# A graph network on one core: one-hot rows made by VectorE, four to a comparison, in place of ScalarE

## The chip, the cores and the metric

One core of a Trainium2 chip runs the whole program. The metric is the device time of one execution in microseconds (us). TensorE is PE in the rows, VectorE DVE, ScalarE ACT, GpSimd POOL; SyncE (SP) issues most transfers.

## The reference

12500 nodes with 128 features, 200000 edges `(src, dst)` sorted by `dst`. Three layers add up neighbours' rows, then one attention layer weights them; layer norms close both parts.

```python
def _L0_gnn_ref(h, src, dst, W1, b1, W2, b2, eps):
    for l in range(W1.shape[0]):                      # three layers
        agg = jax.ops.segment_sum(h[src], dst, num_segments=n)
        z = (1.0 + eps[l]) * h + agg
        hid = jnp.maximum(z @ W1[l] + b1[l], 0.0)
        h = hid @ W2[l] + b2[l]
    return h

def _L1_gnn_ref(h, w, a, src, dst):
    hi, hj = h[src], h[dst]
    e = jnp.matmul(jax.nn.leaky_relu(jnp.matmul(jnp.concatenate([hi, hj], -1), w), 0.2), a)
    exp_e = jnp.exp(e)
    att = exp_e / jax.ops.segment_sum(exp_e, src, num_segments=N)[src]
    return jax.ops.segment_sum(hi * att, dst, num_segments=N)

x = _layernorm(x + _L0_gnn_ref(...))
x = _layernorm(x + _L1_gnn_ref(...))
```

## The kernel before

The nodes lie in 98 windows of 128; their running sums stay in SBUF as `agg`, features on partitions, nodes along the free dimension. The edges lie in tiles of 128 which belong to one window each, except one tile in 16 (the first of a turn) that may reach into the next window. 1568 tiles make 98 turns of 16; a turn is four quads of four tiles. There are four stages that gather: three layers (first rows of `x`, then of `table_g`), then the scores (rows of `table_p`); a last stage of 104 turns gathers little. Between the layers PE, ACT and DVE make the next table by blocks of four windows, and SP stores it.

In a layer the engines work on a tile in this order:

- SP refills the indices (L560) and POOL issues one indirect transfer per tile (L766), which brings 128 rows into a ring of 32 slots. At every fourth gather POOL waits until the quad that had the slots has been multiplied (`rows_used`).
- ACT makes the tile's one-hot matrix from `rel_t`, each edge's place in its window: |iota - rel| by L923 (one instruction per tile), then relu(1 - that) for a quad at once by L933, and by L932 for the second 128 columns of a turn's first tile. L941 copies a turn's 16 columns of `rel_t` with the sign turned. The one-hots go to `span_hot`, four buffers of a quad (`IN_HAND`).
- PE multiplies the rows with the one-hots into PSUM (L1178), a quad in two banks, after waits for DVE's additions, for the one-hots (L1174, L1176) and for the rows.
- DVE adds each tile's sums into its window of `agg` (L1585; L1589 for a turn's second window). It loads 8 window numbers at a time into registers (L468), and for each addition a step of its sequencer (L1562) multiplies the window by 128 and writes the address. Each addition waits for the one before.

In the scores DVE and ACT work on the gathered rows and SP keeps them in HBM; POOL's ring slots come free by SP's L599. PE uses window numbers there. In the last stage DVE weights (L1818, L1829), makes a low part's one-hots (L1810) and adds 16 tiles per turn (L1571), again with addresses made by L1562. Order on each engine is the order of the code; loops are hardware loops.

Of the kernel before, what the change touches and what calls it, by code (L numbers as in the profile page):

```python
# [81 lines left out]
FIRST_A = LAYERS * T2  # L82
# [32 lines left out]
def gnn(nc, x, src, dst, w1, b1, w2, b2, eps, w, a, out):  # L115
    ctx = ExitStack()
    with ctx:
# [34 lines left out]
        def per_tile16(at):  # L152
# [56 lines left out]
        span_at = 6 * QROWS  # L209
        span_away = [big[:, span_at + k * QUAD * 2 * P:span_at + (k + 1) * QUAD * 2 * P].rearrange("p (t n) -> p t n", t=QUAD)  # L210
                     for k in range(2)]
        assert span_at + 2 * QUAD * 2 * P <= CHUNKS * PW
# [48 lines left out]
        one_col = sb("one_col", [P, 1], f32)  # L261
        rel_now = sb("rel_now", [P, TPI], f32)
# [74 lines left out]
        iota_ps = ps[7][:, 0:P]  # L337
        a_ps = ps[6][:, 0:PW]
# [35 lines left out]
        rel_set = sem("rel_set")  # L374
        span_ready = sem("span_ready")
# [14 lines left out]
        hot_ready = sem("hot_ready")  # L390
        rows_used = sem("rows_used")
# [67 lines left out]
        USED = RING  # L459

# [5 lines left out]
        def load_windows(first, engine, n=HALF, of=tile_win):  # L466

            _, values = nc.values_load_multi_w_load_instructions(  # L468
                of[0:1, ds(first, n)], engines=(engine,), min_val=0, max_val=WINS - 1,
                skip_runtime_bounds_check_because="a tile's window, by its making")  # L470
            return list(values)

        def sums_at(q, j):

            return ps[2 * q + j // 2][:, (j % 2) * 2 * P:(j % 2 + 1) * 2 * P]
# [51 lines left out]
        def _(sp):  # L527
# [186 lines left out]
        def _(pool):  # L714
# [137 lines left out]
        def _(act):  # L852
# [61 lines left out]
            def one_hots(l):  # L914

                def distances(turn, q):

                    quad = turn * IN_HAND + q
                    act.wait_ge(hot_ready, 2 + l * QUADS2 + quad - 1)
                    for j in range(QUAD):  # L920
                        t = q * QUAD + j
                        wide = 2 * P if t == 0 else P
                        ins = act.activation(span_away[q % 2][:, j, 0:wide], iota_w[:, 0:wide], ACT.Abs, bias=rel_now[:, t:t + 1])  # L923
                    ins.then_inc(span_ready, 1)

                def hots(turn, q):

                    quad = turn * IN_HAND + q
                    act.wait_ge(span_ready, l * QUADS2 + quad + 1)
                    act.wait_ge(rows_used, USED + l * T2 + quad * QUAD - (IN_HAND - 1) * QUAD)  # L930
                    if q == 0:
                        act.activation(span_hot[q][:, 0, P:2 * P], span_away[q % 2][:, 0, P:2 * P], ACT.Relu, bias=one_col[:, :], scale=-1.0)  # L932
# [3 lines left out]
                with act.Fori(0, TURNS2) as i:  # L936
                    if l:
                        act.wait_ge(span_ready, l * QUADS2 + i * IN_HAND)
                    else:
                        act.wait_ge(hot_ready, 2 + i * IN_HAND)  # L940
                    act.activation(rel_now[:, :], rel_t[:, ds(i * TPI, TPI)], ACT.Copy, scale=-1.0).then_inc(rel_set, 1)  # L941
                    act.wait_ge(rel_set, l * TURNS2 + i + 1)
                    for q in range(IN_HAND):
                        distances(i, q)
                        if q >= 1:
                            hots(i, q - 1)
                    hots(i, IN_HAND - 1)

            act.sem_inc(hot_ready, 2)
            act.wait_ge(g_taken, 2 * QUADS)  # L950
            one_hots(0)
# [4 lines left out]
            one_hots(1)  # L956
            act.wait_ge(added[QUAD - 1], IN_HAND + 2 * QUADS2)
# [4 lines left out]
            one_hots(2)  # L962
            act.wait_ge(added[QUAD - 1], IN_HAND + 3 * QUADS2)
# [128 lines left out]
        def _(pe):  # L1092
            pe.sem_inc(rows_used, USED)
            pe.sem_inc(den_added, 8)
# [71 lines left out]
            def sum_rows(no):  # L1166

                with pe.Fori(0, RINGS2) as i:
                    for t in range(RING):
                        q = (t // QUAD) % IN_HAND  # L1170
                        if t % QUAD == 0:
                            quad = no * QUADS2 + i * (RING // QUAD) + t // QUAD
                            pe.wait_ge(added[QUAD - 1], quad + 1)
                            pe.wait_ge(hot_ready, quad + 3)  # L1174
# [3 lines left out]
                        ins = pe.matmul(sums_at(q, t % QUAD)[:, 0:wide], ring[:, t, :], span_hot[q][:, t % QUAD, 0:wide],  # L1178
                                        start=True, stop=True)
                        if t % QUAD == QUAD - 1:  # L1180
                            ins.then_inc(rows_used, QUAD)
                pe.wait_ge(added[QUAD - 1], (no + 1) * QUADS2 + IN_HAND)
# [149 lines left out]
        def _(dve):  # L1332
            own = Count(dve, dve_own)
            dve.sem_inc(bank_free, HALF)
            for j in range(QUAD):
                dve.sem_inc(added[j], IN_HAND)
# [553 lines left out]
```

## Time and profile before

| | us |
|---|---|
| median of three runs | 9327.69 |
| the runs | 9326.17 to 9331.99 |
| span of the profiled execution | 10761.6 |
| POOL busy in it | 6943.5 |
| PE / DVE / ACT busy in it | 4749.1 / 3994.5 / 3909.3 |

The span runs from the first to the last instruction of one profiled execution; it is 1433.9 us longer than the median of the runs, and all durations below are read from it. Small instructions of an engine's sequencer, such as address steps, are not counted as busy; the chain of work that ended last names them with a q behind the engine (DVEq). "remote" and "another core or an unknown queue" stand for a release whose source the profile does not find.

### The profile page before, as it was taken

To read this page: it belongs to the slowest core of one execution; us is meant where nothing else is said; L and a number is where in the kernel's file an instruction comes from. 1 tells how busy PE (TensorE), PEld (TensorE's weight loads), DVE (VectorE), ACT (ScalarE), POOL (GpSimd) and SP (SyncE) were. 2 spreads that over 40 slices of the span, in tenths; PEclk is the share of its full clock that TensorE was granted. 3 is DMA by queue.
4 is the path that set the end of the run, shared out by engine and by line. 5 is a ranking of instruction groups with operands and counts; after the bars stand their busy time and mean duration, and the time that the engine had idled before them with its cause. 6 is when DMAs were issued, how large, how long until landed. Compare 5 with 4: busy or idle time off the path is not lost.

```text
span 10761.6 us, 137184 instructions
## 1 busy us (share of the span) xinstructions
PE 4749.1 (44%) x27323; PEld 4216.7 (39%) x27324; DVE 3994.5 (37%) x13681; ACT 3909.3 (36%) x11178; POOL 6943.5 (65%) x7392
## 2 busy tenths in 40 slices
PE   3323222343322323342333332256666666667776
PEld 2222222232222222232222222256666666666665
DVE  2222222222222222222222222256556655568888
ACT  3333333333333333333333333322222222237777
POOL 5666666656666666656666666646666666658886
PEclk6555555566555555565555555677778777789998
DMA  3111111122111111121111111145555555544444
GB/s 81 45 46 45 45 46 45 46 59 51 45 45 46 45 46 46 45 65 47 46 45 46 45 46 45 46 139 149 146 147 148 148 147 147 146 132 138 138 139 133
DMA packets 918236, 875.96 MB, mean 81 GB/s; under 512 B 253109, under 2 KB 764001, under 8 KB 918175
## 3 DMA queue, kind: packets, MB, share of 16 engines
q0 software_dynamic: 239728, 516.96, 18.5%
q1 hardware_dynamic: 614765, 259.14, 8.7%
q10 hardware_dynamic: 63698, 99.36, 3.3%
q8 instruction: 15, 0.25, 0.0%
q14 instruction: 30, 0.25, 0.0%
HBM read 734.15 MB, written 137.96 MB: 81 GB/s over the span
## 4 chain that ended last, share of the span: by engine, by line
issue 26%; another core or an unknown queue 23%; DVE 20%; DVEq 17%; PE 11%; ACT 2%; DMA 0%; ACTq 0%; POOL 0%; SPq 0%; POOLq 0%
DVE agg L1585 8%; DVEq L1562 7%; DVEq L468 5%; DVE agg L1571 4%; PE psum L1251 4%; PE psum L1276 2%; DVEq L1580 2%; PE psum L1270 2%; DVE big L1818 2%; DVEq L1593 1%; DVE work L1692 1%; DVE work L1699 1%; PE psum L1178 1%; DVE work L1689 1%
## 5 line engine op out<-in xcount | busy, mean ns | idle before, releaser
L1178 PE MATMUL psum<-work,rows 128*128 128x128 f32 (+1 forms) x9408 | 2056.2, 394 | 4728.1 <-DVE agg L1585 2465.2
L766 POOL DMA_INDIRECT rows<-table_g,idx_now x3136 | 2966.9, 946 | 1688.0 <-issue 1061.4
L1178 PEld LDWEIGHTS psum<-work,rows 128*128 128x128 f32 x9408 | 1825.5, 284 | 4959.6 <-issue 2822.9
L1585 DVE TENSOR_TENSOR agg<-agg,psum 128x128 f32 x4704 | 1351.4, 287 | 5323.6 <-remote 3145.3
L933 ACT ACTIVATE work<-big,one_col 128x512 f32<-128x512 f32 x1176 | 817.9, 710 | 3315.9 <-remote 2837.2
L766 POOL DMA_INDIRECT rows<-in_x,idx_now x1568 | 1483.3, 946 | 799.3 <-issue 467.6
L923 ACT ACTIVATE big<-iota_w,rel_now 128x128 f32<-128x128 f32 (+1 forms) x4704 | 1501.6, 396 | 429.5 <-remote 345.0
L766 POOL DMA_INDIRECT rows<-table_p,idx_now x784 | 764.3, 975 | 480.8 <-SPq L599 254.9
L1010 ACT ACTIVATE work<-psum 128x256 f32<-128x256 f32 x784 | 295.2, 387 | 1864.9 <-remote 1129.9
L1251 PE MATMUL psum<-work 128*128 128x98 f32 x3168 | 624.3, 362 | 689.0 <-DVE work L1692 362.4
L1251 PEld LDWEIGHTS psum<-work 128*128 128x128 f32 x3168 | 569.5, 269 | 741.3 <-DVE work L1692 392.9
L1270 PE MATMUL psum<-big,work 128*128 x3136 | 773.0, 334 | 153.4 <-DVE work L1718 112.3
L766 POOL DMA_INDIRECT work<-table_p,idx_now x588 | 576.3, 980 | 377.2 <-SPq L599 214.5
L1312 PE MATMUL psum<-rows,hot 128*128 128x128 f32 x3328 | 660.4, 326 | 236.9 <-ACT hot L1049 197.2
L1270 PEld LDWEIGHTS psum<-big,work 128*128 128x128 f32 x3136 | 607.5, 240 | 182.2 <-issue 178.5
L1312 PEld LDWEIGHTS psum<-rows,hot 128*128 128x128 f32 x3328 | 496.8, 207 | 382.8 <-ACT hot L1049 250.0
L828 POOL TENSOR_SCALAR hot<-iota_w,big 128x128 f32<-128x128 f32 x624 | 490.4, 790 | 85.1 <-DVE big L1829 63.5
L836 POOL DMA_INDIRECT big<-table_r,idx_now x416 | 412.4, 991 | 147.6 <-issue 99.0
L1571 DVE TENSOR_TENSOR agg<-agg,psum 128x128 f32 x1664 | 476.8, 287 | 51.8 <-PE psum L1312 1.2
L1049 ACT ACTIVATE hot<-big 128x128 f32<-128x128 f32 x1040 | 477.9, 478 | 0.0
L1689 DVE TENSOR_TENSOR work<-psum,hilo 128x392 f32<-128x392 f32 x396 | 222.5, 562 | 556.7 <-remote 406.1
L1699 DVE TENSOR_TENSOR work<-work,psum 128x516 f32<-128x516 f32 x392 | 270.1, 689 | 421.9 <-ACT work L1011 320.8
(211 smaller groups left out, 5718.4 us busy)
## 6 DMA issues: line engine op xcount, KB each, us to landing
rows<-x_of SPq DMA_DIRECT2D x415, 256.0 KB
rows<-table_g,idx_now POOLq DMA_INDIRECT x3136
work<-rel_rows ACTq DMA_DIRECT2D x196, 256.0 KB
x_of<-rows SPq DMA_DIRECT2D x196, 256.0 KB
big<-lo_rows ACTq DMA_DIRECT2D x208, 192.0 KB
x_of<-work SPq DMA_DIRECT2D x147, 256.0 KB
rows<-in_x,idx_now POOLq DMA_INDIRECT x1568
idx_now<-src_t SPq DMA_DIRECT2D x784, 4.0 KB
```

Source lines behind the costliest of these rows:

```text
L468: _, values = nc.values_load_multi_w_load_instructions(of[0:1, ds(first, n)], engines=(engine,), min_val=0, max_val=WINS - 1, skip_runtime ...
L766: pool.indirect_dma_start(out=to, out_offset=None, in_=table, in_offset=bass.IndirectOffsetOnAxis(ap=idx_now[:, at:at + 1], axis=0)) \
L828: pool.tensor_scalar(hot[:, j, :], iota_f[:, :], scalars[:, h, 1, 0, j:j + 1], scalars[:, h, 0, 0, j:j + 1], ALU.is_equal, ALU.mult).then_ ...
L923: ins = act.activation(span_away[q % 2][:, j, 0:wide], iota_w[:, 0:wide], ACT.Abs, bias=rel_now[:, t:t + 1])
L933: act.activation(span_hot[q][:, :, 0:P], span_away[q % 2][:, :, 0:P], ACT.Relu, bias=one_col[:, :], scale=-1.0).then_inc(hot_ready, 1)
L1178: ins = pe.matmul(sums_at(q, t % QUAD)[:, 0:wide], ring[:, t, :], span_hot[q][:, t % QUAD, 0:wide], start=True, stop=True)
L1251: ins = pe.matmul(den_ps, den_hot[:, t % 8, 1, :], den_hot[:, t % 8, 0, 0:HI], start=False, stop=False)
L1270: pe.matmul(sums, hot_t[:, t // QUAD, (t % QUAD) * P:(t % QUAD + 1) * P], q_rows[:, ds(windows[t - h * HALF] * PW, PW)], start=True, stop= ...
L1312: pe.matmul(ps[j // 2][:, (j % 2) * D:(j % 2 + 1) * D], hot[:, j, :], row_of(h * HALF + j, D), start=True, stop=True).then_inc(rows_used, 1)
L1562: dve.lower_ap(to)
L1571: dve.tensor_tensor(to, to, sums, ALU.add).then_inc(bank_free, 1)
L1585: dve.tensor_tensor(to, to, sums_at(q, j)[:, 0:P], ALU.add).then_inc(added[j], 1)
```

## The change

- In the layers DVE makes the one-hots, by comparing a counting row with `rel_t`: one comparison of 128x512 for a quad, and one of 128x128 more for the second window of a turn's first tile. The counting row is copied into PSUM bank 7 ahead of each layer (`iota_2`). ACT has nothing to do in the layers' loops.
- The one-hots for quad q+2 are made just before DVE waits for the sums of quad q; those of the first two quads ahead of the loop. The last turn is taken out of the loop.
- A quad's sums lie in one PSUM bank; a turn's first tile has bank 4 (`IN_HAND`), since it is twice as wide.
- PE counts multiplied quads by a new semaphore, `quads_summed`, one per quad instead of `rows_used` plus 4. It, `added[3]` and `hot_ready` start at such values that PE and DVE wait for the same number at all of them. SP and POOL wait for `quads_summed` in the layers.
- Window numbers are multiplied by 128 once for all tiles (`scale_windows`, one partition, 1664 numbers), ahead of the layers and again ahead of the last stage. DVE loads these and makes the addresses of 8 or 9 tiles at a time. The second window's addition now comes first in its turn.

```diff
-            def one_hots(l):                       # ACT
-                def distances(turn, q):
...
-                        ins = act.activation(span_away[q % 2][:, j, 0:wide], iota_w[:, 0:wide], ACT.Abs, bias=rel_now[:, t:t + 1])
...
-                    act.activation(span_hot[q][:, :, 0:P], span_away[q % 2][:, :, 0:P], ACT.Relu, bias=one_col[:, :],
-                                   scale=-1.0).then_inc(hot_ready, 1)
...
                 def used(lap, lane):               # SP
-                    sp.wait_ge(rows_used, USED + no * T2 + lap * LAP + (lane + 1) * HALF)
+                    sp.wait_ge(quads_summed, Q_USED + no * QUADS2 + lap * (LAP // QUAD) + (lane + 1) * (HALF // QUAD))
...
-                            pool.wait_ge(rows_used, USED - RING + no * T2 + lap * LAP + lane * HALF + j + QUAD)
+                            pool.wait_ge(quads_summed, no * QUADS2 + lap * (LAP // QUAD) + (lane * HALF + j) // QUAD + 1)
...
-                            pe.wait_ge(added[QUAD - 1], quad + 1)
-                            pe.wait_ge(hot_ready, quad + 3)
+                            pe.wait_ge(added[QUAD - 1], Q_USED + quad + 2 - IN_HAND)
+                            pe.wait_ge(hot_ready, Q_USED + quad + 2 - IN_HAND)
...
-                            ins.then_inc(rows_used, QUAD)
+                            ins.then_inc(quads_summed, 1)
...
+            def scale_windows():                   # DVE, this and all below
+
+                own.add(dve.tensor_single_scalar(sums_at_win, tile_win, D.bit_length() - 1, ALU.logical_shift_left))
+                own.wait()
...
+            def one_hots(q, first):
...
+                if q == 0:
+                    dve.tensor_tensor(span_hot[q][:, 0, P:2 * P], iota_2[:, P:2 * P], rel_t[:, ds(first, 1)].to_broadcast([P, P]),
+                                      ALU.is_equal)
+                dve.tensor_tensor(span_hot[q][:, :, 0:P], iota_2[:, 0:P].rearrange("p (o n) -> p o n", o=1).to_broadcast([P, QUAD, P]),
+                                  wide(rel_t[:, ds(first, QUAD)], QUAD), ALU.is_equal).then_inc(hot_ready, 1)
+
+            def add_quad(q, value, sums_to, second_to):
+
+                dve.wait_ge(quads_summed, value)
+                if q == 0:
+                    dve.tensor_tensor(second_to, second_to, sums_at(0, 0, 2 * P)[:, P:2 * P], ALU.add).then_inc(seconds_added, IN_HAND)
+                    dve.wait_ge(seconds_added, value + IN_HAND - 1)
...
+                    to = sums_to[(q % 2) * QUAD + j]
+                    if j:
+                        dve.wait_ge(added[j - 1], value)
+                    dve.tensor_tensor(to, to, sums_at(q, j), ALU.add).then_inc(added[j], 1)
...
+            def sum_turn(l, turn, hots_from):
...
+                    windows = load_sums_at(turn * TPI + h * HALF)
+                    second = load_sums_at(turn + REAL, 1) if h == 0 else []
+                    sums_to = [sums_of(window) for window in windows + second]
+                    for q in range(2 * h, 2 * h + 2):
+                        dve.wait_ge(added[QUAD - 1], values[q])
+                        if q < hots_from:
+                            one_hots((q + 2) % IN_HAND, turn * TPI + (q + 2) * QUAD)
+                        add_quad(q, values[q], sums_to, sums_to[-1])
...
+                own.add(dve.tensor_copy(iota_2, iota_w[:, :]))
+                own.wait()
+                for q in range(2):
+                    one_hots(q, q * QUAD)
+                with dve.Fori(0, TURNS2 - 1) as i:
+                    sum_turn(l, i, IN_HAND)
+                sum_turn(l, TURNS2 - 1, 2)
...
+            scale_windows()                        # also between the scores and the last stage
```

DVE in a layer's loop, a turn's first quad before (ISA is a step of the sequencer; `exp_rel` holds `rel_t`):

```order
L1562 ISA
L1580 ISA [waits rows_used]
L1585 TENSOR_TENSOR agg<-agg,psum 128x128 [waits added3]
L1562 ISA
L1589 TENSOR_TENSOR agg<-agg,psum 128x128 [waits added0]
L1562 ISA
L1585 TENSOR_TENSOR agg<-agg,psum 128x128 [waits seconds_added]
L1562 ISA
L1585 TENSOR_TENSOR agg<-agg,psum 128x128 [waits added1]
L1562 ISA
L1585 TENSOR_TENSOR agg<-agg,psum 128x128 [waits added2]
```

The same quad on DVE in the changed kernel:

```order
L1537 ISA x3
L1556 ISA [waits added3]
L1556 TENSOR_TENSOR work<-psum,exp_rel 128x4x128
L1563 TENSOR_TENSOR agg<-agg,psum 128x128 [waits quads_summed]
L1569 TENSOR_TENSOR agg<-agg,psum 128x128 [waits seconds_added]
L1569 TENSOR_TENSOR agg<-agg,psum 128x128 [waits added0]
L1569 TENSOR_TENSOR agg<-agg,psum 128x128 [waits added1]
L1569 TENSOR_TENSOR agg<-agg,psum 128x128 [waits added2]
```

The address steps have moved ahead of a half turn, and one comparison stands before the wait for the quad's sums.

DVE between the scores and the last stage, in the changed kernel:

```order
L1766 TENSOR_SCALAR exp_rel<-exp_rel 128x98
L1768 COPY src_t<-src_t 128x98 [waits rows_used]
L1771 TENSOR_SCALAR big<-src_t 128x1664 [waits dve_own]
L1529 TENSOR_SCALAR big<-hot 1x1664 [waits dve_own]
L1774 CAST big<-big 128x1664 [waits dve_own]
L1776 COPY idx_now<-src_t 128x2 x2
```

L1529, the scaling of the windows, is new there; the others stood in a row before, as L1768 to L1777.

## Rows read from the trace of the kernel before

**Rows 1.** Layer 0, scores, last stage: length; busy us of PE, PEld, DVE, ACT, POOL.
```profile
77.60:2363.00 2285.40, 684.96 (x3177) 605.88 (x3175) 479.65 (x1675) 812.34 (x2173) 1483.26 (x1568) 0.58 0.18 45
...
7132.50:9627.00 2494.50, 1606.49 (x9670) 1519.10 (x9670) 1479.14 (x3372) 519.42 (x2056) 1531.35 (x1571) 0.78 0.54 145
9627.00:10714.00 1087.00, 849.52 (x7036) 698.43 (x7036) 877.20 (x4562) 817.38 (x2287) 899.97 (x1037) 0.91 0.48 137
```

**Rows 2.** Timeline of POOL in layer 1: start, duration, instruction, idle before.
```profile
3003.15 0.95 POOL L766 DMA_INDIRECT rows<-table_g,idx_now  x1 [0.30 <-issue]
...
3014.41 0.95 POOL L766 DMA_INDIRECT rows<-table_g,idx_now  x1 [0.31 <-issue]
```

**Rows 3.** Timeline of POOL, then of DVE, in the scores.
```profile
8000.96 0.96 POOL L766 DMA_INDIRECT hot<-table_p,idx_now  x1 [0.30 <-issue]
...
8001.15 0.68 DVE L1690 TENSOR_TENSOR work<-psum,hilo 128x512 f32<-128x512 f32 x1
8001.74 0.55 DVE L1692 TENSOR_TENSOR work<-work,psum 128x392 f32<-128x392 f32 x1
```

**Rows 4.** POOL's gathers: durations, first and last start; layers 0, 1, 2, scores.
```profile
L766 POOL DMA_INDIRECT rows<-in_x,idx_now x1568: 942/947/1217, 77.6 to 2345.6; - x196
...
L766 POOL DMA_INDIRECT rows<-table_g,idx_now x1568: 942/947/1457, 2412.1 to 4679.7; - x196
...
L766 POOL DMA_INDIRECT rows<-table_g,idx_now x1568: 942/947/962, 4730.7 to 7000.5; - x196
...
L766 POOL DMA_INDIRECT rows<-table_p,idx_now x784: 954/960/1193, 7132.5 to 9549.2; - x196
L766 POOL DMA_INDIRECT work<-table_p,idx_now x588: 954/960/1199, 7157.9 to 9573.9; - x196
```

**Rows 5.** Who waited for whom, the layers: us in total, times, longest.
```profile
POOL rows L766 <- remote: 935.7, 232, 6.7
```

**Rows 6.** Timeline of all engines in layer 1, a late release.
```profile
3009.60 2.47 PE L1178 MATMUL psum<-work,rows 128*128 128x256 f32 x8 [13.69 <-issue]
...
3018.16 1.25 DVE L1585 TENSOR_TENSOR agg<-agg,psum 128x128 f32 x4 [8.80 <-remote]
```

**Rows 7.** Chain of work, layer 1, a slow stretch and a fast one: start, us, what.
```profile
3008.32 0.70 DVEq L1562
...
3029.30 0.07 DVEq L1562
```

**Rows 8.** The same chain over one undisturbed turn of DVE, first and last.
```profile
3027.97 0.14 issue
...
3035.71 0.65 issue
```

**Rows 9.** Timeline of DVE between the scores and the last stage.
```profile
9616.03 1.03 DVE L1773 TENSOR_SCALAR big<-src_t 128x1664 int32<-128x1664 int32 x1
```

**Rows 10.** Timeline of ACT ahead of layer 0, making its weights.
```profile
96.26 0.28 ACT L889 ACTIVATE w<-psum 128x128 f32<-128x128 f32 x1 [11.51 <-remote]
```

**Rows 11.** Timelines of ACT and DVE between layers 0 and 1.
```profile
2410.88 1.64 ACT L905 ACTIVATE agg<-psum,agg_bias,eps 128x512 f32<-128x512 f32 x2 [0.36 <-PE psum L1201]
...
2443.53 1.89 DVE L1602 CAST big<-big 128x1664 int16<-128x1664 f32 x1 [34.93 <-issue]
...
2448.30 1.03 DVE L1607 CAST big<-big 128x1664 int16<-128x1664 int32 x1
```

**Rows 12.** Timeline of DVE in the last stage.
```profile
10003.70 2.53 DVE L1571 TENSOR_TENSOR agg<-agg,psum 128x128 f32 x8
```

**Rows 13.** Timeline of the scores, then of POOL beside DVE's L1607.
```profile
8021.64 0.48 DVE L1718 TENSOR_SCALAR work<-work,node_c 128x512 f32<-128x512 int16 x1
8021.88 1.07 POOL L766 DMA_INDIRECT work<-table_p,idx_now  x1 [0.30 <-issue]
...
8023.25 1.15 POOL L766 DMA_INDIRECT work<-table_p,idx_now  x1 [0.30 <-issue]
...
2448.69 1.46 POOL L766 DMA_INDIRECT rows<-table_g,idx_now  x1 [0.30 <-issue]
```

More of the change, by code:

```diff
@@ L208, in gnn @@
         assert QUAD * ROW + QROWS <= 2 * T2
[L209 to L212, printed above, removed]
+        sums_at_win = big[0:1, CHUNKS * PW - QROWS:CHUNKS * PW].bitcast(i32)
+        assert max(6 * QROWS, rest_at + HI + P) <= CHUNKS * PW - QROWS
         e_src = rows[:, 0:QROWS].bitcast(i32).rearrange("p (r e) -> p r e", r=RG)
@@ L337, in gnn @@
         iota_ps = ps[7][:, 0:P]
+        iota_2 = ps[7][:, 0:2 * P]
         a_ps = ps[6][:, 0:PW]
@@ L390, in gnn @@
         hot_ready = sem("hot_ready")
+        quads_summed = sem("quads_summed")
         rows_used = sem("rows_used")
@@ L459, in gnn, with load_windows, load_sums_at, sums_at @@
         USED = RING
+        Q_USED = RING // QUAD
         def stand_alone(eng):
             eng.sem_inc(passed, 1)
-        def load_windows(first, engine, n=HALF, of=tile_win):
+        def load_windows(first, engine, n=HALF):
             _, values = nc.values_load_multi_w_load_instructions(
-                of[0:1, ds(first, n)], engines=(engine,), min_val=0, max_val=WINS - 1,
+                tile_win[0:1, ds(first, n)], engines=(engine,), min_val=0, max_val=WINS - 1,
                 skip_runtime_bounds_check_because="a tile's window, by its making")
             return list(values)
-        def sums_at(q, j):
-            return ps[2 * q + j // 2][:, (j % 2) * 2 * P:(j % 2 + 1) * 2 * P]
+        def load_sums_at(first, n=HALF):
+            _, values = nc.values_load_multi_w_load_instructions(
+                sums_at_win[0:1, ds(first, n)], engines=(DVE_E,), min_val=0, max_val=(WINS - 1) * D,
+                skip_runtime_bounds_check_because="D times a tile's window, by its making")
+            return list(values)
+        def sums_at(q, j, wide=P):
+            if q == 0 and j == 0:
+                return ps[IN_HAND][:, 0:wide]
+            return ps[q][:, j * P:j * P + wide]
         def n_chunks(b):
@@ L1335, in _ @@
             for j in range(QUAD):
-                dve.sem_inc(added[j], IN_HAND)
+                dve.sem_inc(added[j], Q_USED + (j == QUAD - 1))
+            dve.sem_inc(seconds_added, Q_USED)
+            dve.sem_inc(hot_ready, Q_USED + 1 - IN_HAND)
             dve.sem_inc(score_ready, 2)
@@ L1591, in layer_sums, with wide @@
-            def layer_sums(l):
-                with dve.Fori(0, TURNS2) as i:
-                    for h in range(2):
-                        windows = load_windows(i * TPI + h * HALF, DVE_E)
-                        second = load_windows(i + REAL, DVE_E, 1) if h == 0 else None
-                        for q in range(2 * h, 2 * h + 2):
-                            add_quad(l, i, q, windows, second)
+            def one_hots(q, first):
+                def wide(col, n):
+                    return col.rearrange("p (t o) -> p t o", o=1).to_broadcast([P, n, P])
+                if q == 0:
[3 more added lines that the diff above has]
+                                  wide(rel_t[:, ds(first, QUAD)], QUAD), ALU.is_equal).then_inc(hot_ready, 1)
@@ new lines, in sum_turn @@
+            def sum_turn(l, turn, hots_from):
+                values = [Q_USED + l * QUADS2 + turn * IN_HAND + q + 1 for q in range(IN_HAND)]
+                for value in values:
+                    dve.compute_val(value)
+                for h in range(2):
+                    windows = load_sums_at(turn * TPI + h * HALF)
[6 more added lines that the diff above has]
+                        add_quad(q, values[q], sums_to, sums_to[-1])
@@ L1822, in weights_of @@
                 dve.lower_ap(given)
-                windows = load_windows(added_next * HALF, DVE_E) if added_next is not None else None
+                windows = load_sums_at(added_next * HALF) if added_next is not None else None
                 dve.wait_ge(hot_act, len(HOT_ACT) * (group + 1))
```

69 lines of the change are left out of this document (12 added, 57 removed).

## The prediction

> **What bounds the kernel now.** I read the busy shares of the page first (POOL leads with 65% of the span), then the busy time by stage, then for each stage the engine whose pace equals the stage's length, and what it waits for. By stage [rows 1] POOL does the same 1483 us in each layer of 2285 us, and 1531 us of the 2494 us of the scores; in the last stage DVE has 877 of 1087 us and follows itself without a gap.
>
> In the layers POOL issues one gather of 128 rows per tile. While it waits for nobody the starts are (3014.41 - 3003.15) / 9 = 1.251 us apart, 0.95 us of it busy and 0.30 us between two [rows 2]. In the scores it is 0.96 + 0.30 = 1.26 us [rows 3]. From the first to the last start a layer takes 2345.6 - 77.6 = 2268.0, 4679.7 - 2412.1 = 2267.6 and 7000.5 - 4730.7 = 2269.8 us, the scores 9573.9 - 7132.5 = 2441.4 us [rows 4], 9246.8 us in all. At its own pace POOL needs 3 x 1567 x 1.251 + 1567 x 1.26 = 7855.3 us. So the profiled execution holds 1391.5 us of waiting of the gathers; in the layers 935.7 us, in 232 pieces, is POOL's idle time that ended with a release whose source the profile does not name [rows 5].
>
> What those waits look like: PE starts the last 8 matmuls before one at 3009.60 and is through after 2.47 us, yet DVE, which waits for that count, starts its additions at 3018.16, 6.1 us later [rows 6]. Before that DVE's sequencer took 0.70 us for each address step that takes 0.07 us elsewhere [rows 7]. In an undisturbed stretch a whole turn of 16 tiles (loads, 17 additions, branch) takes DVE 3035.71 - 3027.97 = 7.7 us [rows 8], against 16 x 1.251 = 20.0 us of POOL.
>
> **Profile against runs.** The page gives no time of the profiled execution but its span, 10761.6 us, and the median of the runs is 9327.69 us: 1433.9 us shorter. Take the gathers' waits out of the span and 10761.6 - 1391.5 = 9370.1 us is left, 0.45% above the median. I read this as follows: the slow stretches are there only while the execution is profiled, and in the timed runs POOL issues gather after gather in all three layers and in the scores. The trace cannot prove it; it is the choice on which the forecast stands.
>
> The Trainium skill ("Runtime: NRT & Kernel Launch", The ~15µs preamble/postamble breakdown) says a profile's total exceeds the execution's time by a constant of about 6.2 us. This case's trace disagrees, with 1433.9 us. By that rule the waits would be part of the timed runs, and rivals 1 and 2 would be the cases to choose between; the measured median decides against it.
>
> **The change, part by part.**
>
> *ACT's one-hots go* (L923, L932, L933, L941 of before: 17 distances, 5 activations and a copy per turn). ACT was never what POOL waited for in an undisturbed stretch, so this is worth 0. What could be late instead is DVE.
>
> *DVE makes them.* Per turn four comparisons of 128x512 with one operand in PSUM and one broadcast column from SBUF, and one of 128x128. The nearest row is L1690, the same form and size: 0.68 us, and the next starts 0.60 us later [rows 3]. 4 x 0.60 + 0.29 = 2.7 us per turn, so a turn becomes 7.7 + 2.7 = 10.4 us, still half of POOL's 20.0. The cover is the gather of the next quad, 4 x 1.251 = 5.0 us per quad against 2.6 of DVE. Were it gone, 2.7 us x 294 turns = 794 us would show. The address steps become fewer (17 of L1562 and one of L1580 per turn before, 6 of L1537 and five before comparisons now); each is 0.07 us beside the addition before it. 0.
>
> *Waits.* DVE now puts the comparison for quad q+2 ahead of its wait for the sums of quad q. Queued behind it are four additions, and PE waits for the last. PE can be three quads ahead of DVE's additions instead of four: one-hots for quad q+2 exist only when DVE has reached q. With 5.0 us between landings and some 1 us of matmuls per quad, one quad ahead is enough. SP's refill of indices and POOL's reuse of ring slots wait for the same event, counted in quads. 0.
>
> *Start of the layers.* Layer 0: DVE's scaling of the windows (nearest row L1773, on 128 partitions and as long, 1.03 us [rows 9]), the copy of the counting row into PSUM (128x256, so under the 0.68 us of a 128x512) and the first comparisons (0.29 + 2 x 0.60) come after ACT's weights, which in the trace are released late, at 96.26 [rows 10]. With some 1.5 us for ACT's copies and as much for DVE's part the first quad's one-hots are there at about 100. POOL comes to reuse its first slot at 77.6 + 32 x 1.251 = 117.6. Layer 1: ACT made one-hots beside DVE's four conversions (L1602 to L1607, 2443.53 to 2449.33 [rows 11]); now they come behind them, at about 2451.5, and POOL wants its first slot at 2412.1 + 40.0 = 2452.1. In this trace that cover is gone by a microsecond. But ACT's 25 blocks ahead of it end late: at the 1.64 + 0.36 = 2.0 us for two of the row at 2410.88, with 23 left, they would end near 2434, not 2443.5, and 9 us of cover remain. Estimate 0, at most 2 us.
>
> *Scores and last stage.* PE still loads plain windows. DVE scales the windows once more between the two stages, on its path: 1.03 us [rows 9], 1.1 with its wait. In the last stage each of 1664 additions loses a multiplication in an address step, but eight additions take 2.53 us, 0.32 each, with the step of 0.07 beside the addition before [rows 7, 12]. So DVE's data path sets the end, but for the first of eight: 0, and at most the two steps ahead of it, a third shorter each, 0.02 us x 2 x 208 halves = 8 us gained.
>
> **Sum.** Against the profiled execution without its waits: 9370.1 + 1.1 = 9371.2; on the median, 9327.7 + 1.1 = 9328.8 us, bounds of these terms -8 and +3.
>
> **Rivals.**
>
> 1. *The slow stretches are in the timed runs too, and fewer address steps shorten them* (faster). For it: DVE's share of the slow chain is address steps, and the change drops a third of them. Against it: 9370.1 lies so near the median, and the count of PE is late where DVE is idle, at ACT's wait of 11.51 us ahead of layer 0 as well [rows 10]. If all went: 9327.7 - 935.7 = 8392 us; if a fifth: 9141 us.
>
> 2. *They are in the timed runs, and three quads in hand bear a late release worse than four* (slower). The waits would grow by 4/3: 935.7 / 3 = 312 us, 9640 us. It decides only if releases of over 3 quads, 15 us, are common without a profiler; those shown here are of 6.1 and 11.5 us [rows 6, 10].
>
> 3. *The comparisons hold POOL up* (slower). For it: gathers beside L1718, a comparison of the same size, took 1.07 and 1.15 us instead of 0.96, and beside L1607 1.46 instead of 0.95 [rows 11, 13]. At 0.11 to 0.19 us for each of 1176 comparisons that is 129 to 223 us on POOL's path: 9457 to 9551 us; the row of 1.46 is of a conversion half as long again. Against it: beside L1690, with one operand in PSUM, a gather took 0.96 [rows 3], as without it. The slowed ones stand beside operations with all operands in SBUF. It decides as soon as one comparison delays one gather, since POOL has no slack.
>
> 4. *DVE becomes the bound* would need over 20 us per turn where 10.4 are worked out: not given a chance of its own.
>
> **Chances.** My forecast 0.71, rival 1 0.16, rival 2 0.05, rival 3 0.06, and 0.02 for a start of a layer or a slower last stage that costs over 0.2%. A difference of 0.2% (19 us) is about what a measurement of this kernel can tell from none. So faster 0.16, same 0.71, slower 0.13. The forecast's own range is 9316 to 9338. To leave out no more than 2 in 10 the range reaches down to a fifth of rival 1's gain, 9141, and up to the low price of rival 3, 9457.
>
> **What would show it.** In the profile after: L1556 at about 0.68 us and gathers beside it at 0.95 (rival 3: over 1.05); undisturbed turns of DVE of about 10.4 us, and POOL's starts 1.251 apart in them; ACT empty in the layers. The span may well fall or rise by hundreds of us, if the slow stretches change with DVE's steps, while the timed median stays: that would confirm the reading of the profile. Should the median fall by over 100 us, the gathers' waits were real and the step "Profile against runs" is wrong; should it rise by 100 us or more, ask whether gathers got longer (rival 3) or only further apart (rival 2).

## The result, and the profile after

| us | median | lowest to highest |
|---|---|---|
| before | 9326.93 | 9324.65 to 9331.99 |
| after | 9572.09 | 9567.06 to 9574.13 |

The ratio is 1.0262, 95% interval 1.0247 to 1.0276: 245 us slower. The forecast was 9328.8 us, with a range that ended at 9457; the prediction was wrong.

The busy time by stage shows where the time is. Columns: stretch, its length, busy us of PE, PEld, DVE, ACT and POOL, granted clock of TensorE, DMA share, GB/s; the rows are layer 0, the scores and the last stage [rows 1].

```profile
77.10:2046.00 1968.90, 999.59 (x3190) 758.54 (x3189) 770.31 (x2168) 8.18 (x19) 1480.50 (x1568) 0.50 0.19 53
...
6172.60:8190.00 2017.40, 1438.97 (x9634) 1352.52 (x9634) 1472.02 (x3360) 534.75 (x2056) 1515.78 (x1568) 0.85 0.66 180
8190.00:9522.00 1332.00, 976.35 (x7072) 829.74 (x7072) 877.67 (x4573) 816.93 (x2287) 899.43 (x1040) 0.78 0.39 112
```

The layers and the scores run at POOL's pace, with none of the waits of [rows 4, 5]: the gathers of layer 0 start from 77.1 to 2034.2, (2034.2 - 77.1) / 1567 = 1.249 us apart, and take 0.944 us each beside VectorE's new comparisons of 0.69 us. From POOL's gathers and DVE's comparisons by line (count, shortest/median/longest in ns, first and last start):

```profile
L772 POOL DMA_INDIRECT rows<-in_x,idx_now x1568: 940/944/1545, 77.1 to 2034.2; - x196
...
L1556 DVE TENSOR_TENSOR work<-psum,exp_rel x1176: 678/691/693, 88.2 to 6035.1; 128x512 f32<-128x512 f32 x196
```

The last stage grew from 1087 to 1332 us while every engine but PE was busy for the same time. By its additions, first and last start, it took 1323.6 us here and 1082.2 us in a second profile of the kernel before (e7 below): 241 of the 243 us between these two executions.

```profile
L1546 DVE TENSOR_TENSOR agg<-agg,psum x1664: 269/286/290, 8199.2 to 9522.8; 128x128 f32 x185
```

The groups of DVE by line tell where it stood still. Columns: busy us, mean ns | idle us before and what ended it. First the weights' product in the kernel before (L1829), then the same in the kernel after (L1828):

```profile
L1829 DVE TENSOR_TENSOR big<-big,exp_rel 128x32 f32<-128x32 f32 x208 | 40.4, 194 | 122.7 <-issue 80.3 <-DVE big L1818 39.2 <-ACT hot L1049 1.7
```

```profile
L1828 DVE TENSOR_TENSOR big<-big,exp_rel 128x32 f32<-128x32 f32 x208 | 40.3, 194 | 374.5 <-issue 369.7 <-ACT hot L1015 1.9 <-DVE big L1817 1.7
```

Idle time ahead of it rose by 374.5 - 122.7 = 252 us, 1.2 us for each of 208 halves (a half is eight tiles of a turn). The chain of work shows one such gap (start, us, what; q is the engine's sequencer). Its record of the load, `DVEq L472`, is cut at the next data instruction:

```profile
9003.62 0.19 DVEq L472
9003.81 0.24 DVE big L1817 x2
9004.05 1.45 issue
9005.50 0.04 DVEq L1823
```

The load's own rows, durations in ns (shortest/median/longest), in the first profile of the kernel before, in its second (e7) and after: the loads of window numbers into DVE's registers, 882 in the layers, a third of them of one number, and 208 of eight numbers in the last stage.

```profile
L468 DVEq TENSOR_LOAD <-hot x1090: 6/600/1394, 85.0 to 10710.8; - x182
```

```profile
L468 DVEq TENSOR_LOAD <-hot x1090: 303/598/625, 84.4 to 9276.6; - x182
```

```profile
L472 DVEq TENSOR_LOAD <-big x1090: 305/1846/3162, 88.3 to 9518.4; - x182
```

Eight numbers now take 1.85 us where they took 0.60. One number takes 0.31 in both. No line of the change looks like it: it loads as many numbers, by the same instruction. What differs is the place and the writer of the numbers.

```diff
         tile_win = hot_mem[0:1, QUAD * ROW:QUAD * ROW + QROWS].bitcast(i32)
+        sums_at_win = big[0:1, CHUNKS * PW - QROWS:CHUNKS * PW].bitcast(i32)
```

### The profile page after: what moved, and what is told of

Same layout as the page of the kernel before. It is cut to its first block, busy times and chain, and to the rows that moved or that the text cites. A ratio compares the mean times of both kernels' runs of the same rounds, so it can differ in the third digit from the quotient of the medians.

```text
span 9570.4 us, 125651 instructions
## 1 busy us (share of the span) xinstructions
PE 5605.7 (59%) x27323; PEld 4602.3 (48%) x27324; DVE 4855.9 (51%) x15155; ACT 1529.9 (16%) x4710; POOL 6917.0 (72%) x7392
## 4 chain that ended last, share of the span: by engine, by line
POOL 61%; issue 25%; DVE 8%; DVEq 1%; PE 1%; POOLq 1%; DMA 1%; ACT 1%; SPq 0%; ACTq 0%
POOL rows L772 53%; POOL work L772 6%; DVE agg L1546 5%; DVE big L1817 2%; POOL hot L772 2%; PE psum L1154 0%; DVEq L1817 0%; POOLq L784 0%; ACT work L1052 0%; POOLq L461 0%; DVEq L472 0%; PE psum L1168 0%; PE psum L1177 0%; DVE work L1664 0%; DVE stats L1633 0%
## 5 line engine op out<-in xcount | busy, mean ns | idle before, releaser
L1145 PE MATMUL psum<-work,rows 128*128 128x128 f32 (+1 forms) x9408 | 2953.6, 470 | 2890.0 <-DMA rows<-table_g,idx_now 1323.9
L1145 PEld LDWEIGHTS psum<-work,rows 128*128 128x128 f32 x9408 | 2246.3, 322 | 3597.5 <-DMA rows<-table_g,idx_now 1231.3
L1556 DVE TENSOR_TENSOR work<-psum,exp_rel 128x512 f32<-128x512 f32 x1176 | 809.8, 689 | 991.2 <-issue 903.7
L1279 PE MATMUL psum<-rows,hot 128*128 128x128 f32 x3328 | 747.0, 373 | 353.3 <-ACT hot L1015 332.7
L1279 PEld LDWEIGHTS psum<-rows,hot 128*128 128x128 f32 x3328 | 592.2, 253 | 491.1 <-ACT hot L1015 351.4
L1237 PE MATMUL psum<-big,work 128*128 x3136 | 715.2, 314 | 110.9 <-ACT work L977 59.2
L1237 PEld LDWEIGHTS psum<-big,work 128*128 128x128 f32 x3136 | 564.0, 224 | 128.3 <-issue 127.5
L1243 PE MATMUL psum<-rows,ident 128*128 128x129 f32 x1568 | 373.9, 325 | 222.3 <-DMA rows<-table_p,idx_now 221.4
L1218 PE MATMUL psum<-work 128*128 128x98 f32 x3168 | 490.8, 308 | 4.8 <-DVE work L1690 4.7
L1015 ACT ACTIVATE hot<-big 128x128 f32<-128x128 f32 x1040 | 477.7, 478 | 0.0
L1218 PEld LDWEIGHTS psum<-work 128*128 128x128 f32 x3168 | 471.9, 228 | 6.7 <-DVE work L1690 5.6
```

The lines of the kernel that those rows point to most:

```text
L1015: act.activation(hot[:, j, :], away[:, n % 2, :], ACT.Relu, bias=scalars[:, h, 0, 0, j:j + 1], scale=scalars[:, h, 0, 1, j:j + 1]).then_in ...
L1145: ins = pe.matmul(sums_at(q, t % QUAD, wide), ring[:, t, :], span_hot[q][:, t % QUAD, 0:wide], start=True, stop=True)
L1218: ins = pe.matmul(den_ps, den_hot[:, t % 8, 1, :], den_hot[:, t % 8, 0, 0:HI], start=False, stop=False)
L1237: pe.matmul(sums, hot_t[:, t // QUAD, (t % QUAD) * P:(t % QUAD + 1) * P], q_rows[:, ds(windows[t - h * HALF] * PW, PW)], start=True, stop= ...
L1243: ins = pe.matmul(sums, ident[:, :], wide_quads[(u * TPI + t) // QUAD][:, t % QUAD, 0:PW], start=False, stop=True)
L1279: pe.matmul(ps[j // 2][:, (j % 2) * D:(j % 2 + 1) * D], hot[:, j, :], row_of(h * HALF + j, D), start=True, stop=True).then_inc(rows_used, 1)
```

## Experiments

The theory, P: this alignment decides how many accesses the load is split into. The rivals, B: `big` is a slow place, being far along the partition and read by others. V: numbers written by VectorE, or the extra address instruction, make it slow.

**e1_by_64**

```diff
-        sums_at_win = big[0:1, CHUNKS * PW - QROWS:CHUNKS * PW].bitcast(i32)
...
+        sums_from = CHUNKS * PW - QROWS - 2
+        sums_at_win = big[0:1, sums_from:sums_from + QROWS].bitcast(i32)
...
```

> The changed kernel with one number changed: the table of scaled window numbers begins two words (8 bytes) earlier in big, so that each load of eight numbers begins at a multiple of 32 bytes (the table itself at a multiple of 64) and not 8 bytes behind one. In the changed kernel this load takes 1.85 us in place of 0.60, and lies on VectorE's path 208 times in the last stage; a load of one number takes 0.31 us in both kernels. Theory P (the start within a few bytes decides how many accesses the load is split into): the load falls to 0.60 us or below; last stage 1332 -> about 1080 us, total 9572 - 208 x 1.25 = 9312 to 9327; if it falls to 0.3 us, up to 62 us less again, 9265. Theory B (the tensor big, far into the partition and read by other engines, is the slow place): nothing changes, 9572. Theory V (the numbers are written by VectorE and not by a transfer, or the address is computed in one instruction more): nothing changes, 9572.

Measured: 9314.26 us against 9331.03 of the kernel before on the same chip, ratio 0.9982 (0.9973 to 0.9991). Two words less, and 245 us are back and 17 more: against the changed kernel's 9572.09 us, on another chip, 258. The load, L1829 and the last stage's additions (1066.6 us from first to last start, against 1323.6):

```profile
L473 DVEq TENSOR_LOAD <-big x1090: 303/596/1277, 88.6 to 9273.5; - x182
```

```profile
L1829 DVE TENSOR_TENSOR big<-big,exp_rel 128x32 f32<-128x32 f32 x208 | 40.3, 194 | 117.1 <-DVE big L1818 114.6 <-DMA big<-table_r,idx_now 1.4 <-ACT hot L1016 0.7
```

```profile
L1547 DVE TENSOR_TENSOR agg<-agg,psum x1664: 269/287/291, 8210.2 to 9276.8; 128x128 f32 x185
```

The place, the writer and the instructions are those of the changed kernel, so B and V fall. The load stays at 0.60: a multiple of 32 gives nothing beyond a multiple of 16.

**e2_by_16** (the same with `- 6` in place of `- 2`)

> As the run before, but the table begins six words earlier: every load of eight numbers begins 16 bytes behind a multiple of 32, as in the kernel before. Theory P: the load takes the 0.60 us of the kernel before, total 9312 to 9327. If this run and the one before differ, the finer start (32 bytes) matters too. Theories B and V: 9572.

Measured: 9315.84 us, ratio 0.9983 (0.9973 to 0.9992), load 0.597 us. The same as e1.

**e3_before_off**

```diff
-        tile_win = hot_mem[0:1, QUAD * ROW:QUAD * ROW + QROWS].bitcast(i32)
...
+        tile_win = hot_mem[0:1, QUAD * ROW + 2:QUAD * ROW + 2 + QROWS].bitcast(i32)
...
```

> The kernel before with one number changed: its table of window numbers begins two words further in hot, so that each load of eight begins 8 bytes behind a multiple of 16, as in the changed kernel. Nothing else of the change is in it. Theory P: the load takes 1.85 us in place of 0.60 on VectorE and TensorE, the layers and scores hide it, and the last stage grows by 208 x 1.25 = 260 us at most, measured 245 in the changed kernel: 9327 + 245 = 9572. Theories B and V: 9327.

Measured: 9582.79 us, ratio 1.0269 (1.0253 to 1.0284). The kernel before, with nothing of the change in it, gets the whole loss from two words. TensorE's loads in the scores suffer too (L468 on PEldq, the median of 294 loads of which a third are of one number: 591 ns before, 2410 here). It cost nothing there: the gathers of the scores start from 6184.8 to 8175.1, in 1990.3 us, and in e7 from 6172.2 to 8165.6, in 1993.4.

```profile
L468 DVEq TENSOR_LOAD <-hot x1090: 305/1848/2311, 84.6 to 9543.0; - x182
```

**e4_table** (the essence; `probe` begins at a multiple of 64 bytes)

```diff
...
+            for off in range(16):
+                timed(off, 8)
+            for off in (0, 1, 2, 4):
+                for n in range(1, 9):
+                    timed(off, n)
```

> The changed kernel, with 48 loads into VectorE's registers appended behind its last work, from a place that begins at a multiple of 64 bytes: eight numbers from word 0 to word 15, and one to eight numbers from words 0, 1, 2 and 4. Each loaded number is then used once. Only the durations of the loads are looked at. Theory P: the eight-number load takes 0.60 us or less at words 0, 4, 8 and 12 and 1.85 us at the others (or at words 1 to 3 and so on), repeating every four or every eight words; the duration grows with the count of numbers by steps at word 2 and little at word 0. Theories B and V: the eight-number load takes the same at each word. Total: the 9572 of the changed kernel plus some 48 x 5 us.

Measured: 9704.72 us, and these durations of the loads in ns:

| numbers | 1 | 2 | 3 | 4 | 5 | 6 | 7 | 8 |
|---|---|---|---|---|---|---|---|---|
| from word 0 | 317 | 543 | 745 | 349 | 628 | 840 | 1042 | 605 |
| from word 1 | 311 | 536 | 741 | 960 | 1184 | 1401 | 1622 | 1841 |
| from word 2 | 310 | 527 | 739 | 956 | 1184 | 1405 | 1626 | 1841 |
| from word 4 | 316 | 542 | 745 | 359 | 606 | 834 | 1043 | 605 |

In the first part of the table eight numbers from words 4, 8 and 12 took 610, 604 and 605 ns, and from every word not divisible by four 1841 to 1847 (the very first load, from word 0, took 916 behind other work). In the chain, four numbers from word 0, then four from word 1:

```profile
9635.10 0.35 DVEq L1877
```

```profile
9650.87 0.96 DVEq L1877
```

So a load costs about 0.31 us and 0.22 us for each further number, except that four numbers which begin at a multiple of 16 bytes come together. A load that doesn't begin there takes all of its numbers one by one, also those that would lie well. The Trainium skill ("Advanced Engine Details and Errata", SBUF Cachelines) speaks of lines of 16 bytes in SBUF; the table agrees with that size, and no run shows that these lines are the reason. The Trainium skill ("Runtime: NRT & Kernel Launch", Instruction fetch mechanics) gives about 200 ns per register for TENSOR_LOAD even in bulk, where it speaks of loads from HBM; the rows from words 1 and 2, loaded from SBUF, lie near it with 0.22, and eight aligned numbers, 0.60 in all, do not.

**Where the other 17 us come from.** With aligned loads the changed kernel is faster than before by more than the 8 us at most of the prediction. I took the last stage's shorter address steps for the cause and split the change.

**e5_last_alone** (the kernel before, last stage with the scaled, aligned table)

```diff
-                to = sums_of(window)
+                to = sums_of(window, 1)                # without the multiplication by D
...
+            scale_windows()                            # ahead of the last stage only
...
-                windows = load_windows(added_next * HALF, DVE_E) if added_next is not None else None
+                windows = load_sums_at(added_next * HALF) if added_next is not None else None
```

> The kernel before with one part of the change alone: in the last stage the window numbers come already multiplied by 128, from a table at a multiple of 64 bytes. The layers are those of the kernel before, ScalarE's one-hots included. In the changed kernel with its table at a multiple of 64 bytes a turn of the last stage took 10.31 us against 10.47 (0.10 of it behind the loop's jump, the rest in shorter address steps), 104 turns: 16 us. Theory L (all of the gain of that run lies in the last stage): 9331 - 16 = 9315, ratio 0.998. Rival: the gain is that of the layers, and this run stands at 9331, ratio 1.000.

**e6_layers_alone** (the kernel after, aligned, with the last stage of before)

```diff
-                windows = load_sums_at(added_next * HALF) if added_next is not None else None
+                windows = load_windows(added_next * HALF, DVE_E) if added_next is not None else None
...
-                to = agg[:, ds(window, D)]
+                to = agg[:, ds(window * by, D)]    # by: 1 in the layers, D in the last stage
```

> The other part alone: the changed kernel's layers (VectorE's one-hots, loads from a table at a multiple of 64 bytes), and the last stage of the kernel before, which loads plain window numbers and multiplies them in its address steps. Theory L (the layers are bound by GpSimd's issues, one each 1.25 us, so VectorE's one-hots are worth nothing there): 9331, ratio 0.999 to 1.001. Rival: 9315, ratio 0.998.

The comments behind `#` in the cuts of e5 to g2 are explanations and not in the code.

Measured: e5 9327.39 against 9328.32, ratio 1.0001 (0.9992 to 1.0010); e6 9313.93, ratio 0.9985 (0.9976 to 0.9994). My theory L fell: it is the run with the layers' part alone that has the gain. But the time is not saved in the layers. The last stage's additions, first and last start, of the kernel before (profiled again, e7 below), e5, e6 and f1 (below):

```profile
L1571 DVE TENSOR_TENSOR agg<-agg,psum x1664: 269/286/291, 8197.6 to 9279.8; 128x128 f32 x185
```

```profile
L1585 DVE TENSOR_TENSOR agg<-agg,psum x1664: 268/286/290, 8201.2 to 9279.6; 128x128 f32 x185
```

```profile
L1547 DVE TENSOR_TENSOR agg<-agg,psum x1664: 271/286/290, 8194.7 to 9264.0; 128x128 f32 x185
```

```profile
L1548 DVE TENSOR_TENSOR agg<-agg,psum x1664: 271/286/291, 8197.0 to 9197.9; 128x128 f32 x185
```

That is 1082.2, 1078.4, 1069.3 and 1000.9 us. e6 gains 12.9 us in a stage whose code is that of before. The chain behind the jump back of that stage's loop shows it, in the kernel before and in g1 (below), which has the gap of e6 too; the rows are the jump, the gap, and the loop's first register step:

```profile
8729.14 0.06 DVEq L1844
8729.19 0.25 issue
8729.44 0.06 DVEq L1844
```

```profile
8718.91 0.06 DVEq L1846
8718.97 0.14 issue
8719.11 0.06 DVEq L1846
```

0.25 against 0.14 us, 102 times: 11 us. The changed kernel has the 0.14 as well. In e6 this loop begins at the 1252nd instruction of DVE's program and before at the 1154th, because the layers' code ahead of it has grown. The next two runs test the place alone.

**g1_before_98** and **g2_by_64_157** (the first in the kernel before, the second in e1)

```diff
             dve.wait_ge(agg_scaled, BLOCKS)
             dve.wait_ge(info_in, 32)
+            for _ in range(196):                   # 314 in g2; two waits make one instruction
+                dve.wait_ge(agg_scaled, BLOCKS)
```

> The kernel before, with 98 instructions more in VectorE's program ahead of the first layer's loop, each of which waits for something long reached (two waits in each) and costs some 0.05 us once, where VectorE waits for the first rows anyway. They move the last stage's loop from the 1154th to the 1252nd instruction of VectorE's program, which is where it stands in the kernel with the layers' part alone (9314); nothing else changes. Theory J (behind the jump back of the last stage's loop VectorE's sequencer needs 0.25 us in the kernel before and 0.14 in the changed one, by the place of the loop in its program; 102 times 0.11 us): 0.14 us here too, 9328 - 11 = 9317. Rival K (what precedes the loop, or how the registers are set, makes the difference): 0.25 us, 9328 to 9333. The jump in the scores' loop, which GpSimd hides, should go from 0.14 to 0.24 us by theory J, since it comes to stand where it does in the changed kernel.

> The changed kernel with its table at a multiple of 64 bytes, with 157 such instructions more ahead of the first layer's loop. The last stage's loop moves from the 1253rd to the 1410th instruction, 256 behind the 1154th, where it stood in the kernel before. Theory J, with a period of 256 instructions or a divisor of it: 0.25 us behind the jump, 9314 + 11 = 9325. If the place matters in another way than by that period, 0.14 us and 9314 to 9320. Rival K: 0.14 us, 9314 to 9320.

Measured: g1 9315.19 us, ratio 0.9987 (0.9978 to 0.9996); g2 9325.03, ratio 0.9997 (0.9988 to 1.0006), with 0.24 us behind the jump. Theory J holds on both sides: 98 instructions that do nothing make the kernel before 13 us faster, and 157 more take most of the gain from e1, whose last stage grows from 1066.6 to 9276.9 - 8199.4 = 1077.5 us. The jump in the scores' loop turned as expected too, to 0.24 us in g1. The idle time ahead of the first weighting instruction of a half, before, g1, g2:

```profile
L1818 DVE SCALAR_TENSOR_TENSOR big<-iota_w,big,psum 128x98 f32<-128x98 f32 x1248 | 312.7, 313 | 36.4 <-issue 34.7 <-PE psum L1296 1.7
```

```profile
L1820 DVE SCALAR_TENSOR_TENSOR big<-iota_w,big,psum 128x98 f32<-128x98 f32 x1248 | 312.7, 314 | 24.5 <-issue 22.7 <-PE psum L1296 1.7
```

```profile
L1820 DVE SCALAR_TENSOR_TENSOR big<-iota_w,big,psum 128x98 f32<-128x98 f32 x1248 | 312.7, 313 | 36.5 <-issue 34.8 <-PE psum L1264 1.7
```

Why a place is the quick one is open. In these kernels DVE's loops from instructions 1252, 1253 and 1256 had 0.14 us in the last stage and those from 1154, 1155 and 1410 had 0.24 or 0.25; the scores' loop had 0.14 us from 1005 and 1260, and 0.24 from 1103. The layers' loops, which POOL's pace hides, counted in the same built programs, had 0.14 us from 287, 294, 385, 424, 483 and 554, and 0.22 to 0.25 from 451, 581 and 711 (all three in g2, the one from 581 in g1 too). Neither the distance from the program's start nor the remainder of the place when divided by four sorts these. The Trainium skill ("Advanced Engine Details and Errata", Sequencer Memory) names an instruction cache with lines of 256 bytes; no run here shows that it is the cause.

**e7_before_again** (the kernel before, unchanged)

> The kernel before, unchanged, profiled once more. In its first profile GpSimd's transfers waited 1391.5 us and the span was 1434 us above the median of the runs. A kernel that differed only in the place of the window numbers had a span 12 us above its median and no slow stretch. Theory C (the slow stretches were an accident of that one profiled execution): span 9330 to 9345, layers' stages about 1970 us each. Rival: profiling this kernel always brings them, span above 10000, and the place of the numbers had taken them away.

Measured: 9329.21 us, and the profile of that same execution has a span of 9327.4 us. The slow stretches of the first profile are gone, its layer 0 and its last stage are

```profile
77.30:2045.50 1968.20, 997.24 (x3179) 756.74 (x3179) 478.71 (x1672) 838.74 (x2173) 1479.44 (x1568) 0.50 0.19 53
...
8188.00:9279.80 1091.80, 849.94 (x7072) 697.72 (x7072) 879.38 (x4580) 817.07 (x2287) 899.78 (x1040) 0.92 0.48 136
```

**f1_one_copy** asks what sets the last stage's pace, by shortening DVE's sequencer at the cost of its data path (on top of e1):

```diff
+                own.add(dve.tensor_copy(hi_now[:, :], hi_t[:, ds(group * HALF, HALF)]))    # once per half, ahead of the additions
...
-                    ins = dve.scalar_tensor_tensor(chosen[:, j, :], iota_f[:, 0:HI], hi_t[:, ds(group * HALF + j, 1)], of,
+                    ins = dve.scalar_tensor_tensor(chosen[:, j, :], iota_f[:, 0:HI], hi_now[:, j:j + 1], of,
```

Each half's weighting also waits for the copy (`own.wait`).

> The changed kernel with its table at a multiple of 64 bytes, and in the last stage one addition: ahead of each half VectorE copies the half's eight comparison numbers (128x8) to a fixed place, so that its six weighting instructions need no address step each. Theory S (VectorE's own sequencer sets the half: six address steps at 0.16 us, the load at 0.60, the waits behind it at 0.41, against 1.43 us of data path): five steps less give some 0.35 us back, up to the 0.5 us that the data path idles there, the copy takes 0.1 to 0.2: 208 x 0.15 to 0.3 = 30 to 60 us less than 9314, 9255 to 9285. Rival D (the data path sets the half): 208 x 0.1 to 0.2 more, 9335 to 9355.

Measured: 9247.31 us, ratio 0.9914 (0.9901 to 0.9928), 81 us faster than the kernel before. The stage of 1066.6 us in e1 (last of its additions at 9276.8, first at 8210.2) takes 1000.9 here. The copy adds 33 us to DVE's data path, and yet the stage shrinks by 66; the idle time ahead of the weights' product falls from 117.1 to 24.8 us:

```profile
L1831 DVE TENSOR_TENSOR big<-big,exp_rel 128x32 f32<-128x32 f32 x208 | 40.5, 195 | 24.8 <-DVE big L1820 19.1 <-DMA big<-table_r,idx_now 1.4 <-POOL hot L836 0.2
L1838 DVE COPY hi_now<-big 128x8 f32 (+1 forms) x208 | 33.1, 159 | 0.0
```

The product still waits for the weighting's result there, so that wait alone was not what held it for 117.1 us in e1. It is the fastest of the kernels here.

## Why the prediction was wrong

**The step that failed** is "Scores and last stage": "So DVE's data path sets the end, but for the first of eight: 0". It held for the eight additions and was carried to the whole half. Between the last weighting instruction and the product the data path stood still for 122.7 us in the trace of before, and for 122.5 in e7; "follows itself without a gap", said of [rows 1], was not true. The profile of before puts 80.3 of it down to "issue", that of e7 120.6 to L1818, the weighting's own result, so the releaser named does not decide it. f1 does: less work for the sequencer and more for the data path made the stage 66 us shorter. There the sequencer sets the pace, and on it lay the load of eight numbers. Not in every half: of the chain over e7's last stage ACT's one-hots (L1049) have 5.8% and PE's matmuls (L1312) 5.3%.

And the load had no term in the sum at all: the change moved the table it reads, I costed the instructions that the change removed from around it, and took its duration as given. Its term measures 208 x 1.25 = 260 us as an upper bound. By the timed medians 258 came through in the changed kernel (9572.09 - 9314.26, on two chips) and 252 in e3. The loss of 245 us is this less some 13 us that the new place of the last stage's loop gave and up to 4 from shorter address steps. This was a price that no row of before showed for an unaligned start, but the load itself, 0.60 us in a chain with idle time behind it, should have been a term with a range.

The outcome, a slower last stage, lay in the last 0.02 of the chances, without a mechanism. The sign that the prediction gave for a rise of 100 us or more pointed at the gathers, which got neither longer nor further apart.

**TensorE's clock** moved with it. The granted clock, a mean over stretches at its two levels of 1.2 and 2.4 GHz (0.5 and 1.0), was 0.91 in the last stage of before and 0.78 after, with PE's busy time at 976 in place of 850 us; e7 has 0.92 and 850 us, and f1, with the shortest halves, 0.97. After, PE's matmuls L1279 wait 332.7 us for ACT's one-hots (L1015), and ACT 502.6 us for DVE's product (L1828); PE's wait for ACT was 212.2 us in e7. So I take the lower clock for a result of the longer halves. That it cost nothing of its own was not tested.

```profile
8187.00:9197.90 1010.90, 795.29 (x7072) 649.63 (x7072) 910.26 (x4787) 817.04 (x2287) 899.46 (x1040) 0.97 0.52 147
L1279 PE MATMUL psum<-rows,hot 128*128 128x128 f32 x3328 | 747.0, 373 | 353.3 <-ACT hot L1015 332.7 <-DVE agg L1546 3.1
  ACT idx_now L1000: 502.6, 205
L1312 PE MATMUL psum<-rows,hot 128*128 128x128 f32 x3328 | 658.7, 326 | 239.2 <-ACT hot L1049 212.2 <-DVE agg L1571 1.1 <-POOL hot L828 0.2
```

These are the last stage of f1, then PE's matmuls and who waited for L1828 after, then PE's matmuls in e7.

**The profile against the runs.** The forecast rested on the reading that the timed runs hold none of the 1391.5 us of waits. That is right: the medians and two clean profiles (spans of 9570.4 and 9327.4 us beside 9572.14 and 9329.21 us of the same executions) say so. The cause given for it, that this kernel has the slow stretches whenever it is profiled, is not right: profiled again, it has none. They were an accident of that one profiled execution; whether the profiler can bring them on, and what made them, is open. So this step of the prediction had the right conclusion with some luck, and rivals 1 and 2 had no object. The constant that the prediction quotes from the Trainium skill is not met by the clean profiles either: their spans, from first to last instruction, are 1.7 and 1.8 us below the execution's time, not 6.2 above. The Trainium skill speaks there of the profile's total, which no view here gives.

**The layers: worth 0,** as said. The gathers of layer 0 start from 77.1 to 2034.2 after and, in e7, from 77.3 to 2033.4, in 1957.1 and 1956.1 us. The row of e7:

```profile
L766 POOL DMA_INDIRECT rows<-in_x,idx_now x1568: 940/944/992, 77.3 to 2033.4; - x196
```

ACT is empty (8.18 us in layer 0, against 838.74) and DVE has 770 in place of 479 us, 3.0 us per turn more, against 2.7 in the prediction. Two loads per turn that were 1.25 us longer each, which the prediction did not know of, were hidden as well.

**Rival 3** (comparisons hold POOL up) fell: the gathers' median is 944 ns after and in e7. **Three quads in hand** and the moved starts cost nothing that the pace of the gathers shows: the scaling of the windows took 1.02 us each time, and between layers 0 and 1 the gathers pause from 2034.2 to 2091.8 after, and from 2033.4 to 2091.5 in e7.

**The shorter address steps** were bounded at 8 us. e5, with its 1082.2 - 1078.4 = 3.8 us in the stage, agrees; the timed medians, 0.9 us apart, can't tell it from none. The other 13 us are not of the change's work, but of where it put the loop.

## What to carry to other kernels

Let a table of which registers are loaded in groups begin at a multiple of 16 bytes, and load in multiples of four: two words of offset were worth some 250 us here, and no line of the code looks slower. When a diff moves an operand, price the instruction that reads it anew, even where that instruction is unchanged; and read the idle time between an engine's data instructions before saying that its data path sets the pace, since a few sequencer steps of 0.1 us in a loop are worth more than a copy of 0.16. A gain or loss of 0.1% in a kernel with short hardware loops can come from where the loop stands in its engine's program, so pad the program to the same place before crediting it to an edit.

## What the runs showed of the hardware

- A register load of eight numbers from SBUF takes 0.60 us at a multiple of 16 bytes and 1.84 us otherwise; four take 0.35 and 0.96, one takes 0.31 (e4). In the changed kernel it took 1.85 us in the layers, where the loops of the other engines don't touch `big`, and in the last stage, where they do.
- On TensorE's sequencer the median of the scores' loads, two of three of them of eight numbers, was 2.41 us unaligned (e3) and 0.59 aligned (before).
- The Trainium skill ("DMA: Bandwidth & Descriptors", Latency and other measured facts) gives about 600 ns as the floor of `tensor_load`. The trace's TENSOR_LOAD of one number from SBUF took 0.31 us here, of four aligned ones 0.35.
- Behind a loop's jump DVE's sequencer needed 0.14 us or 0.22 to 0.25 us, by the loop's place in the program.
- One profile in twelve held slow stretches, 1.4 ms in all, with sequencer steps of 0.70 in place of 0.07 us; no other did.
